# PE's order in the attention loop: two tiles of keys at a time, value matmuls of both behind the scores of both

## What is computed

```
qh = (q @ Wq.T + bq).reshape(b, t, h, d).transpose(0, 2, 1, 3)
kh = (k @ Wk.T + bk).reshape(b, -1, h, d).transpose(0, 2, 1, 3)
vh = (v @ Wv.T + bv).reshape(b, -1, h, d).transpose(0, 2, 1, 3)
attn = jax.nn.softmax(jnp.einsum('bhtd,bhsd->bhts', qh, kh) * scale, axis=-1)
out = jnp.einsum('bhts,bhsd->bhtd', attn, vh)
```

## Time and profile before

| | |
|---|---|
| median of 3 runs | 2705.45 us (2705.42 to 2705.73) |
| the profiled execution | 2710.2 us |
| its span, first to last instruction | 2708.1 us |
| PE busy | 2494.6 us, 92% of the span |
| DVE busy | 2161.4 us, 80% |
| ACT busy | 1939.4 us, 72% |

### The profile page before, as it was taken

The page is one execution under the profiler, slowest core; times in us unless marked ns, Lnnn a source line. Parts: engine busy times, 40 slices in busy tenths (PEclk is TensorE's granted clock), DMA queues, the critical chain, the costliest instruction groups (busy, mean ns, idle before and its releaser), DMA issues.

```text
span 2708.1 us, 51412 instructions
## 1 busy us (share of the span) xinstructions
PE 2494.6 (92%) x21338; PEld 967.9 (36%) x21340; DVE 2161.4 (80%) x2211; ACT 1939.4 (72%) x3545; POOL 41.2 (2%) x28
## 2 busy tenths in 40 slices
PE   2389999999999999997893899999999999999979
PEld 1243333333333333343441333333333333333334
DVE  5468999999999999944434899999999999999234
ACT  2058888888888888874330188888888888888932
POOL 4000000000000000000010000000000000000000
PEclk8559999999999999999895699999999999999989
DMA  7120000000000000003101000000000000000010
GB/s 251 68 78 23 29 29 29 27 28 28 29 29 29 28 28 28 20 32 113 63 0 61 11 27 28 29 29 29 29 28 28 28 29 29 29 29 14 2 63 8
DMA packets 38612, 102.86 MB, mean 38 GB/s; under 512 B 4164, under 2 KB 14936, under 8 KB 38120
## 3 DMA queue, kind: packets, MB, share of 16 engines
q1 hardware_dynamic: 36936, 99.14, 10.0%
q10 hardware_dynamic: 1440, 0.40, 0.1%
HBM read 83.72 MB, written 15.80 MB: 37 GB/s over the span
## 4 chain that ended last, share of the span: by engine, by line
PE 64%; DVE 29%; SPq 3%; DMA 3%; issue 1%; ACT 1%; POOL 1%; ACTq 0%; DVEq 0%; POOLq 0%
DVE m_part L657 26%; PE ps L976 23%; PE ps L928 19%; PE ps L947 10%; PE ps L1074 4%; PE ps L1082 3%; SPq L297 2%; PE ps L888 1%; DMA q_parts<-probs 1%; PE ps L918 1%; SPq L306 1%; DMA probs<-in_mask_t 1%; PE ps L880 1%; PE ps L995 1%; DVE probs L613 1%
## 5 line engine op out<-in xcount | busy, mean ns | idle before, releaser
L657 DVE TENSOR_REDUCE m_part<-ps 128x2 f32<-128x1024 f32 (+1 forms) x1664 | 1933.7, 1184 | 209.0 <-PE ps L947 199.7
L495 ACT ACTIVATE probs<-ps 128x512 f32<-128x512 f32 (+1 forms) x3264 | 1763.8, 595 | 325.2 <-PE ps L928 213.6
L976 PE MATMUL ps<-probs,v_all 128*9 128x256 f32 x13056 | 1014.2, 383 | 1.7 <-ACT o_raw L475 0.5
L928 PE MATMUL ps<-q_ring,k_ring 35*128 35x512 f32 x3264 | 871.1, 498 | 0.6 <-ACT q_ring L484 0.4
L947 PE MATMUL ps<-k_ring,q_ring 33*128 33x512 f32 (+1 forms) x3328 | 733.7, 420 | 94.6 <-DVE m_part L657 36.2
L928 PEld LDWEIGHTS ps<-q_ring,k_ring 35*128 35x128 f32 x3264 | 349.5, 183 | 697.2 <-ACT probs L495 603.3
L947 PEld LDWEIGHTS ps<-k_ring,q_ring 33*128 33x128 f32 x3328 | 350.9, 194 | 183.2 <-DVE m_part L657 110.1
L976 PEld LDWEIGHTS ps<-probs,v_all 128*9 128x9 f32 x13056 | 195.3, 89 | 551.4 <-ACT probs L495 466.0
L792 DVE TENSOR_TENSOR probs<-probs,k_ring 128x512 f32<-128x512 f32 x64 | 43.6, 691 | 64.9 <-ACT probs L528 56.6
L678 DVE RECIPROCAL r_den<-ps 128x8 f32<-128x8 f32 x32 | 6.6, 207 | 110.6 <-PE ps L955 110.6
L482 ACT ACTIVATE q_ring<-ps 3x512 fp32r<-3x512 f32 x32 | 18.8, 587 | 102.2 <-PE ps L918 101.5
(11 more groups left out here) (122 smaller groups left out, 598.3 us busy)
## 6 DMA issues: line engine op xcount, KB each, us to landing
k_ring<-k_parts SPq DMA_DIRECT2D x384, 96.0 KB
k_ring<-k_parts SPq DMA_DIRECT2D x128, 112.2 KB
k_ring<-gate_rows SPq DMA_DIRECT2D x16, 512.0 KB, 7.3
probs<-in_mask_t SPq DMA_DIRECT2D x10, 640.0 KB, 4.4
k_parts<-probs SPq DMA_DIRECT2D x12, 512.0 KB, 3.1
k_parts<-big SPq DMA_DIRECT2D x12, 512.0 KB, 3.1
q_ring<-q_parts SPq DMA_DIRECT2D x128, 32.0 KB
big<-in_w SPq DMA_DIRECT2D x1, 2048.0 KB, 10.7
```

Source lines behind the costliest of these rows:

```text
L495: A(probs[0:k, n % PSLOTS, HALF * half:HALF * half + HALF], ps[0:k, e_bank(unit), :], ACT.Exp, scale=SCALE).then_inc(sem(f"exp_done{l}"), 1)
L657: V.tensor_reduce(m_part[:, h % 2, :, p, c], mx(n % 2)[:, :, 0:chunk_w[c]], AX.X, ALU.max).then_inc(sem(f"mx_done{l}"), 1)
L928: pe.matmul(bank, k_ring[row:row + ROWS_EXP, koff:koff + P], q_ring[row:row + ROWS_EXP, qoff:qoff + HALF], start=not masked, stop=True).th ...
L976: mm = pe.matmul(ps[32 * g:32 * g + VW, 7, 0:QGW], v_all[:, t, h, :], probs[:, n % PSLOTS, QGW * g:QGW * g + QGW], start=(t == 0), stop=(t ...
```

## The change

`attention` now looks at the steps of a head two at a time. A step is *plain* if it has two scores and exactly one unit, a maximum unit. If t is even and t and t + 1 are both plain, and the layer isn't masked, PE issues:

1. both scores and the maximum unit of t, as before;
2. the score of half 0 of t + 1, then the wait for the unit's banks, then the maximum matmul of half 1 and that of half 0 of t + 1 (in that order, the second raising `mx_filled`), then the score of half 1 of t + 1;
3. the value matmuls of t - 2 and of t - 1, each with the warming matmuls that belong to it.

All other steps are as before. The order on ACT, DVE and SP is not touched, nor the numbers that the semaphores count to. The diff, cut:

```
-            def max_tile(l, n, h, j, masked):
+            def max_tile(l, n, h, j, masked, halves=range(2), done=True):
...
-                for half in range(2):
+                for half in halves:
...
-                mm.then_inc(sem(f"mx_filled{l}"), 1)
+                if done:
+                    mm.then_inc(sem(f"mx_filled{l}"), 1)
...
+                def plain(h, t):
+                    units = max_units(h)[t]
+                    return len(units) == 1 and units[0][0] == "max" and len(score_units(h)[t]) == 2
+
+                def fill_pair(h, t):
+
+                    fill(h, t)
+                    (first, second), ((_, of, j),) = score_units(h)[t + 1], max_units(h)[t + 1]
+                    n = UNIT_AT["max", of, j]
+                    score(l, first, masked)
+                    pe.wait_ge(sem(f"mx_done{l}"), n - 1)
+                    max_tile(l, n, of, j, masked, (1,), False)
+                    max_tile(l, n, of, j, masked, (0,), True)
+                    score(l, second, masked)
...
                 for h in range(H):
...
+                    for t in range(NT):
+                        if not masked and t % 2 == 1 and plain(h, t - 1) and plain(h, t):
+                            weigh_behind(h, t - 1)
+                            weigh_behind(h, t)
+                            continue
+                        if not masked and t % 2 == 0 and t + 1 < NT and plain(h, t) and plain(h, t + 1):
+                            fill_pair(h, t)
+                            continue
+                        fill(h, t)
                         if l == 0 and h == H - 1 and t >= 4 + LAG and (t - LAG) % 4 == 0:
                             next_layer((t - LAG) // 4 - 1)
...
+                        weigh_behind(h, t)
```

More of the change, by code:

```diff
@@ L1012, in attention, with fill @@
                         score(l, ("rows", 0, 0), masked)
-                for h in range(H):
[L1014 to L1018, removed]
+                def fill(h, t):
+                    for unit in score_units(h)[t]:
+                        score(l, unit, masked)
+                    for unit in max_units(h)[t]:
+                        m_unit(l, unit, masked)
@@ new lines, in weigh_behind @@
+                def weigh_behind(h, t):
+                    n = h * NT + t - LAG
+                    if n >= 0:
+                        weigh(l, n // NT, n % NT)
+                        for _ in range(dense(n // NT, n % NT)):
+                            keep_warm()
+                for h in range(H):
+                    for t in range(NT):
[7 more added lines that the diff above has]
+                        fill(h, t)
```

## The result

The change makes the kernel slower: 3268 us median of four executions (3249 to 3307), against 2705.6 before. The ratio is 1.205, with a 95% interval of 1.199 to 1.212. The forecast was 2849, with a range up to 2880; the direction was right, the size wrong by more than 400 us.

A forecast was written before the change was run, and what follows sets the result against it. PE's own order (1.22 us a step) and the score-exp-score loop (1.25) were taken to bound the kernel; extra time over 608 pairs summed to 144 us, giving 2849 us median (2854 profiled), range 2814 to 2880.

The forecast's parts named there:

- The loop closed inside the pair: In each pair the fourth score needs the first score's bank, so it waits for that exp: 0.60 + 0.60 + 0.05 = 1.25 us.
- s3: Fourth score of a pair, half 0 of its second tile, forecast to load 1.25 us after the first score.
- The length of a pair: Normal pair on PE: 1.25 + 0.43 + 0.66 + 0.33 = 2.67 us against 2.46, so 0.21 more.
- the rival of 0.33 for the second tile: Second value tile in a pair costs a whole turn, 0.33 for 0.22: 67 us more, 2916 us; 4%.
- the one by which s3's weights come ahead: PE pulls the fourth score's weight load ahead: 0.10 less a pair, some 65 us less in all, 2784 us; 5%.
- The special pairs: Pairs that are not normal: two narrow ones a head at 0.33 more each, (26,27) at 0.60 more, (48,49) at 0.22 more.
- (26,27): Pair of tiles 26 and 27, behind the step with two maximum units: second tile's maxima wait for DVE, 3.05 us, 0.60 more.
- (48,49): Pair of tiles 48 and 49, behind the rows unit, whose exp comes late: 2.93 us against 2.71, 0.22 more.
- narrow ones: Pairs holding a narrow maximum unit (keys of the last chunk): 2.67 us against 2.34, 0.33 more each.
- The rivals that made it faster: Chiefly: PE works on value matmuls while the fourth score waits, 0.19 less a pair, about 2590 us; 3%.
- the paragraph on the granted clock: Clock could fall as PE pauses some 0.2 us in each pair; head 15 waits too at 1.00, so none expected.
- m': Maximum matmuls of a pair's second tile: forecast at 0.58 us, but at 1.39 in (26,27), where they wait for DVE.

The follow-up runs named there:

- the filled pair: The change with all its pairs, plus eight warming matmuls in PE's wait for DVE in pair (26,27) of heads 1 to 13: 2843 us.
- the filled start: The kernel before plus twelve warming matmuls a layer in PE's waits for DVE in steps 1 and 2 of head 0: 2706.3 us, ratio 1.000.
- the version with the early first score: Kernel before, with the next tile's half 0 score issued ahead of the step's value matmuls: 2687 to 2695 us, but 3390 to 3418 in five of eleven executions.

## Why the prediction was wrong, and where it was right

**The loop closed inside the pair: right.** s3 was put at 1.25, its load is at 1.244, and it waits for ACT's exp. The run with short exps moves it to 0.93 as the same sum says.

**The length of a pair: right.** 2.67 forecast, 2.654 measured, which over 608 pairs is most of the 11 us by which the sum came out too high; 0.43 from s3 to the value matmuls and 0.22 for each further pass, also across tiles, were read from the right rows. So the rival of 0.33 for the second tile falls (sixteen value matmuls take 1.05 us in all), and so does the one by which s3's weights come ahead: the Trainium skill's rule on early weight loads (TensorE: Matmul & The Clock Gate, Packing small matmuls) doesn't help a load that carries the wait itself: this one came at 386.62, when the exp was done, and the value matmuls 0.44 later.

**The special pairs: right.** (26,27) 3.05 forecast and 3.03 measured in head 2, (48,49) 2.93 and 2.90, narrow ones 2.67 and 2.65. (A head has three pairs with narrow units, not two; the third, tiles 42 and 43, took 2.46 before like a normal one, so the sum is not touched.) A middle head at full clock takes 70.2, forecast 70.5.

**The rivals that made it faster: didn't happen.** The value matmuls are held behind s3, as in head 15.

**The clock: wrong, and it is the whole error.** The step that failed is the paragraph on the granted clock. It looked at the pause of a normal pair, about 0.2 us, took head 15 as its row, where PE waits for ACT too at a clock of 1.00, and expected no fall. For the normal pairs that was right, as the run without (26,27) shows (1.00 through 1110 us). But the sum itself had put m' of pair (26,27) at 1.39 instead of 0.58 (measured 1.38 in the pair at 441.92), and this pause was priced only by its length, 0.60 us. The runs showed that it lets the clock fall about every second time (17 of 36; 3417 us with it alone), that a longer wait of PE does so in the old order (7 of 7; 3891 us), that filling the pair's wait with matmuls prevents it (0 of 26; 2843 us), and that once low the clock may stay low for over a thousand microseconds of uninterrupted matmuls. Its price was 406 us in the profiled execution, beside the 16 (26 times 0.60) that the sum had for it. There was a stretch to be warned by, in the trace of the kernel before: after the waits of 0.38 and 0.39 us in head 0 its clock is 0.50 from 200 to 205 us (the windows shown above), a fall that happened to end soon. Ten microseconds in a slice of 68 don't show in the earlier trace rows, and I had looked no closer than the slices and one head's mean. A rival "PE's longest pause lets the clock fall, and it stays down" with heads at the low level would have given a time beyond 3000 and belonged among the rivals. And head 15 was no safe row: in two of the thirteen recorded executions (the filled pair and the filled start) the clock falls for 14 and 17 us where head 14 ends and head 15 begins, among steps of its kind.

What stays open: why the same pause of 0.40 us lets the clock fall at one place and not at the next, and why the clock comes back after 10 us in one execution and not for a whole layer in another. The returns stand at or behind the steps with warming matmuls (tiles 3 to 5), near the doubled step (24 and 28) or near the rows step and the end of a head (46 and 50), but most such steps passed without a return, and no run here separates them.

## What to carry to other kernels

Price a new wait on PE twice: by its length, and by what it does to the granted clock. Look for the longest pause in the loop, not the mean one; a pause of 0.4 to 0.9 us in otherwise unbroken matmul work cost 400 to 1200 us here. Eight useless matmuls that filled it gave that back; where they filled a third of it, only part came back. And if a ring of buffers closes a loop once per step, moving two steps' producers into one block closes it inside the block: with three banks the fourth score waits for the first one's consumer, so split the block elsewhere, as the version with the early first score does.

## What the runs showed of the hardware that was not expected

- A full load of PE is not enough to get the clock back: 1372 us with PE recorded busy in all of them went by at 0.50 in the run with one longer wait, 1500 of 1500 us in the recorded run of the version with the early first score.
- At the low level the order of the change is the better one: 4.09 us a pair against 2 x 2.12 for two old steps. The wait for exp is down to 0.09 us there, while one of two turns between value matmuls and scores is still saved.
- DVE's reductions of 1.22 us start 1.13 apart when they queue, so a recorded duration overstates what a unit costs; that part of the forecast held.
